# Local attention layers as a seven-stage pipeline on three rotating bank pairs, with the mask added by VectorE

## The reference, cut to what matters

```
x1 = global_attention(x) + x
y  = layernorm(x1)
for l in range(6):
    t = shift(y)                          # second 64 features come from the token before
    q, k, v = split(t @ Wqkv[l])          # 16 heads of 64
    q, k = l2norm(q)*qs, l2norm(k)*ks;  q, k = rotary(q), rotary(k)
    s = 8 * q_window @ k_window.T         # windows of 32 tokens see 32 before and themselves
    s = where(banned, -max, s);  a = softmax(s)
    y = y + (a @ v_window) @ Wo[l]
    n = layernorm(shift(y)) * g + b
    y = y + ((n @ W1a + b1a) * gelu(n @ W1g + b1g)) @ W2[l] + b2[l]
out = y + x1
```

## Time and profile before

| | |
|---|---|
| median of 3 runs | 3665.57 us (3654.13 to 3666.7) |
| profiled execution | 3663.69 us, its span 3661.9 us |
| TensorE | 3133.4 us busy, 86% of the span; mean granted clock 0.951 |
| VectorE | 2503.8 us, 68% |
| ScalarE | 2070.3 us, 57% |
| GpSimd | 2294.0 us, 63% |
| DMA | 71 GB/s mean; the main queue's packets take 32.4% of 16 engines |

### The profile page before, as it was taken

One profiled execution on the slowest core, in us unless ns is written; L12 is line 12 of the kernel. 1 busy time (PEld: TensorE's weight loads), 2 busy tenths in 40 slices (PEclk: granted clock), 3 DMA queues, 4 the chain that ended last, 5 costly groups with the idle time before them and its releaser, 6 DMA issues. The chain is left out here.

```text
span 3661.9 us, 121537 instructions
## 1 busy us (share of the span) xinstructions
PE 3133.4 (86%) x52983; PEld 2292.0 (63%) x52983; DVE 2503.8 (68%) x3404; ACT 2070.3 (57%) x2481; POOL 2294.0 (63%) x1606
## 2 busy tenths in 40 slices
PE   3499999999999999488888888888888888888885
PEld 2377777777777777256666666666666666666664
DVE  5777777777777774366676666766676667666673
ACT  2255555555555554256666666666666666666663
POOL 1545545454554540577777777777777777777772
PEclk7699999999999999699999999999999999999997
DMA  4645454544445450422223222322222232222221
GB/s 110 104 80 88 80 86 78 87 80 86 84 83 85 81 87 5 133 59 57 53 54 90 61 54 65 77 57 61 75 66 54 61 81 63 54 57 60 54 53 38
DMA packets 277481, 260.20 MB, mean 71 GB/s; under 512 B 106263, under 2 KB 220840, under 8 KB 276824
## 3 DMA queue, kind: packets, MB, share of 16 engines
q1 hardware_dynamic: 275272, 252.05, 32.4%
q10 hardware_dynamic: 1680, 0.40, 0.1%
HBM read 98.30 MB, written 40.37 MB: 38 GB/s over the span
## 5 line engine op out<-in xcount | busy, mean ns | idle before, releaser
L660 ACT ACTIVATE prob<-psS 128x1024 f32<-128x1024 f32 x512 | 524.2, 1024 | 603.0 <-PE psS L537 599.9
L824 DVE TENSOR_TENSOR colmax<-psS,colmax 128x1024 f32<-128x1024 f32 x480 | 587.2, 1223 | 315.3 <-PE psS L537 313.5
L537 PE MATMUL psS<-diag,pst 128*128 128x64 bf16 x16384 | 587.3, 195 | 13.9 <-issue 13.7
L537 PEld LDWEIGHTS psS<-diag,pst 128*128 128x128 f16 x16384 | 520.9, 99 | 74.1 <-issue 20.5
L1266 PE MATMUL R<-wqkv,xsT 128*128 128x512 f32 x1152 | 557.4, 607 | 1.5 <-ACT qT L1402 1.1
L529 PE MATMUL psS<-qst,kst 48*128 48x128 bf16 (+1 forms) x8192 | 382.8, 221 | 143.3 <-DMA pst<-p_parts 85.7
L758 POOL TENSOR_TENSOR rel<-rel,rec 128x1024 f32<-128x1024 f32 x64 | 151.8, 2372 | 510.5 <-DVE rec L837 510.5
L1530 POOL TENSOR_TENSOR pr<-pr,rnq 128x1024 f32<-128x1024 f32 x96 | 182.7, 1903 | 394.7 <-DVE pr L1611 394.7
L529 PEld LDWEIGHTS psS<-qst,kst 48*128 48x128 bf16 (+1 forms) x8192 | 235.6, 95 | 301.5 <-issue 156.6
L571 PE MATMUL psO<-prob,v 128*9 128x128 f32 x8192 | 326.3, 276 | 6.0 <-issue 5.4
L1266 PEld LDWEIGHTS R<-wqkv,xsT 128*128 128x128 f32 x1152 | 198.7, 192 | 164.1 <-issue 162.5
(11 more groups left out here) (190 smaller groups left out, 6341.9 us busy)
## 6 DMA issues: line engine op xcount, KB each, us to landing
v<-vs SPq DMA_DIRECT2D x576, 128.0 KB, 2.4
pst<-p_parts SPq DMA_DIRECT2D x512, 128.0 KB, 4.9
p_parts<-stage SPq DMA_DIRECT2D x64, 512.0 KB, 3.0
v<-vs SPq DMA_DIRECT2D x384, 64.0 KB, 2.0
wqkv<-in_L_ffn_Wqkv SPq DMA_DIRECT2D x18, 512.0 KB
q_stack<-qpart SPq DMA_DIRECT2D x6, 512.0 KB
qst<-q_stack SPq DMA_DIRECT2D x32, 96.0 KB, 5.2
wo<-in_L_ffn_Wo SPq DMA_DIRECT2D x6, 512.0 KB
```

The costliest lines, as they stand in the source:

```text
L537: last = pe.matmul(o, pst[:, par, g, P * jb:P * (jb + 1)], diag[:, par, g, h0:h0 + HH // 2, :], start=False, stop=(g == NG - 1), skip_grou ...
L660: act.activation(prob[:, st % 2, :], psS[:, slot_of("b", st)].rearrange("p a b -> p (a b)"), ACT.Exp)\
L824: dve.tensor_tensor(dst, src, dst, ALU.max).then_inc(a_read, 1)
```

## The change

- The local layers' program is written anew. Step s (from -1 to 101) works on seven units: projections, norms and rotation of s; key and query transposes of s-1; scores, softmax and weighted values of s-2; output transposes of s-3; output projection, residual and norm statistics of s-4; feed-forward 1 and gating of s-5; feed-forward 2 and residual of s-6. The transpose of the input of s+1 is in it as well.
- PSUM: three pairs of banks (`R[0]` to `R[2]`) are handed out in turn to ten uses a step (`RING`), in the order S, Q, kT, K, V, qT, pT, oT, h, O. Each use waits for the reader of the use three before it. The two remaining banks are `psA` (output projection, input transpose) and `psB` (normed input, feed-forward 2).
- The mask is added by VectorE, from PSUM into `pr` in SBUF. The maximum reads `pr` and the subtraction is done in place in `pr`. The two mask products go, and `pr` and q's rotated tile get two buffers.
- The input shift of a projection is done by ScalarE while it copies the transpose out (three copies, one of them a column carried to the next unit); its three DMAs go. The feed-forward shift stays three DMAs, into two buffers.
- Feed-forward 1 has the weights as the stationary side (six products of 128 columns). GELU takes its bias as a per-partition operand, and the bias and gating of the other half are one VectorE operation for each of three pieces. The three transposes, the bias add and the two copies behind them go. The bias comes as six column DMAs instead of one broadcast row.
- In the last layer x1's block is loaded, added by GpSimd and stored block by block. The final blocks go.
- Global attention: the `guard` event is at key block 11 instead of 12 (its DMAs behind block 12, not 13), `max1` is at 9 instead of 10, and VectorE takes events ahead of `a_max`.

```diff
-                ev[8], ev[10], ev[12] = "max0", "max1", "guard"
+                ev[8], ev[9], ev[11] = "max0", "max1", "guard"
...
+                    if jb > 0:
+                        take(unit_events(ul, first, last), jb - 1, it, ul, first, last)
                     if not (last and st + LEAD >= 4 * NB):
                         al, ja = divmod(st + LEAD, NB)
                         a_max(b + LEAD, st, al, ja)
-                    if jb > 0:
-                        take(unit_events(ul, first, last), jb - 1, it, ul, first, last)
...
+        RING = (("S", 2), ("Q", 0), ("kT", 1), ("K", 0), ("V", 0), ("qT", 1), ("pT", 2), ("oT", 3), ("h", 5), ("O", 2))
+        STEPS = range(-1, NT + 6)
+        turns = [(kind, s - lag) for s in STEPS for kind, lag in RING if 0 <= s - lag < NT]
+        slot = {t: i % 3 for i, t in enumerate(turns)}
+        earlier = {t: turns[i - 3] for i, t in enumerate(turns) if i >= 3}
+        read_by = {"S": "masked_done", "Q": "sqq_done", "kT": "kT_ready", "K": "sqk_done", "V": "v_ready", "qT": "qT_ready",
+                   "pT": "pT_ready", "oT": "oT_ready", "h": "g_done", "O": "o_ready"}
...
+    # TensorE, step s: S(s-2) Q(s) kT(s-1) K(s) wo(s-4) xnT(s-5) V(s) qT(s-1) xT(s+1) w2(s-6) pT(s-2) oT(s-3) h(s-5) O(s-2)
+                        pe.wait_ge(m["g_done"], n + 1)
+                        pe.wait_ge(m["xnT_ready"], min(n + 2, NT))
+                        for i, (lo, r) in enumerate(FC):
+                            last = pe.matmul(psB[:, 0:D], gT[0:r, i, :], w2[0:r, n // NB % 2, D * i:D * (i + 1)], ...)
...
+                        for a in range(2):
+                            for i, (lo, r) in enumerate(FC):
+                                last = pe.matmul(R[slot["h", n]][0:r, a, P * i:P * (i + 1)],
+                                                 w1[:, n // NB % 2, FF * a + lo:FF * a + lo + r], xnT[:], start=True, stop=True)
...
+    # ScalarE, step s: kT(s-1) square q(s) exp(s-2) square k(s) V(s) qT(s-1) pT(s-2) oT(s-3) gelu(s-5) xT(s+1)
+    # GpSimd, step s: scale k(s-1), root q(s-1), scale scores(s-2), add q(s), add k(s), xmb(s-6), table(s+1), root k(s), rstd(s-4)
...
+    # VectorE, step s
+                        dve.tensor_tensor(p, scores, allowed, ALU.add).then_inc(m["masked_done"], 1)      # s-2
+                        dve.tensor_reduce(mx[:], p, AX.X, ALU.max).then_inc(m["mx_done"], 1)
+                        dve.tensor_tensor(p, p, mx[:].unsqueeze(2).broadcast_to([P, LH, 2 * WIN]), ALU.subtract)
+                        rotate(n, 0, flat[slot["Q", n]], q1[:, n % 2, :], q2[:], "tq_done")               # s
+                        rotate(n, 1, flat[slot["K", n]], k1[:], k2[:], "tk_done")
+    # then: sum of q squares(s), residual(s-4), scale normed input(s-5), sum of exponentials(s-2), sum of k squares(s),
+    # reciprocal(s-2), residual(s-6), statistics(s-4), divide output(s-2), gate(s-5), normalize(s-4)
+                            last = dve.scalar_tensor_tensor(gT[0:r, i, :], R[slot["h", n]][0:r, 0, P * i:P * (i + 1)],
+                                                            b1_cols[0:r, n // NB % 2, i:i + 1], gl[0:r, i, :], ALU.add, ALU.mult)
+                        dve.tensor_scalar(xn[:], xs_f[:, n % 2, :], mv[:, 0:1], rstd[:, 0:1], ALU.subtract, ALU.mult)
```

More of the change, by code:

```diff
@@ L1257, in _, with free @@
             def _(pe):
-                def turn_x(n, par):
-                    wait(pe, xs_a_dma[par], (n // 2 + 1) * 48)
-                    pe.transpose(flat[1][:, 512:512 + P], xs_a[:, par, :], ident[:]).then_inc(m["xT_done"], 1)
-                def project(n, par, which, bank, done):
-                    w = at(wqkv, wp(n))
+                def free(kind, n):
+                    if (kind, n) in earlier:
+                        before, unit = earlier[kind, n]
+                        pe.wait_ge(m[read_by[before]], unit + 1)
@@ new lines, in turn @@
+                def turn(kind, n, src, done):
+                    o = flat[slot[kind, n]]
+                    for i in range(PAIRS):
+                        last = pe.transpose(o[:, P * i:P * (i + 1)], src[:, P * i:P * (i + 1)], ident[:])
+                    last.then_inc(m[done], 1)
+                for s in STEPS:
+                    n = s - 2
+                    if has(n):
+                        par = n % 2
+                        pe.wait_ge(m["qT_ready"], n + 1)
+                        pe.wait_ge(m["kT_ready"], n + 1)
+                        free("S", n)
+                        o = flat[slot["S", n]]
@@ new lines, in _ @@
+                        last.then_inc(m["s_done"], 1)
+                    n = s
+                    if has(n):
+                        pe.wait_ge(m["xT_ready"], n + 1)
+                        if n % NB == 0:
+                            pe.wait_ge(m["w_dma"], (n // NB + 1) * (16 * NWL))
+                        free("Q", n)
+                        project(n, 0, "Q", "q_done")
+                    n = s - 1
+                    if has(n):
+                        pe.wait_ge(m["kn_done"], n + 1)
+                        free("kT", n)
+                        turn("kT", n, kn, "kT_done")
@@ L1397, in _ @@
-                steps(pe, step)
+                                last = pe.matmul(o[WIN * w:WIN * (w + 1), P * i:P * (i + 1)], prT[:, i, WIN * w:WIN * (w + 1)],
+                                                 v2[:, par, w, :, i, :], start=True, stop=True, skip_group_check=True)
+                        last.then_inc(m["pv2_done"], 1)
             @block.scalar
@@ new lines, in _ @@
+                    n = s - 3
+                    if has(n):
+                        act.wait_ge(m["oT_done"], n + 1)
+                        if n > 0:
+                            act.wait_ge(m["wo_done"], n)
+                        copy(otT[:].rearrange("p a b -> p (a b)"), flat[slot["oT", n]], "oT_ready")
+                    n = s - 5
+                    if has(n):
+                        act.wait_ge(m["h_done"], n + 1)
+                        if n > 0:
+                            act.wait_ge(m["g_done"], n)
+                        for i, (lo, r) in enumerate(FC):
+                            last = act.activation(gl[0:r, i, :], R[slot["h", n]][0:r, 1, P * i:P * (i + 1)], ACT.Gelu,
+                                                  bias=b1_cols[0:r, n // NB % 2, 3 + i:4 + i])
+                        last.then_inc(m["gelu_done"], 1)
```

791 lines of the change are left out of this document (358 added, 433 removed).

## The result

| | median | ratio to before, 95% interval |
|---|---|---|
| before | 3659.85 us (3652.94 to 3666.7, 4 runs) | |
| after | 3406.81 us (3399.55 to 3418.45, 4 runs) | 0.9312 [0.9276, 0.9347] |

What follows compares the result with a forecast made beforehand. Interlocking engines bound the local step: chain and GpSimd loop 19.0 us, taken as 19.05, over TensorE's 17.2 floor. Periods -254, global attention -30, start -7, end -25, weight loads +4 sum to -312: 3352 us, range 3265 to 3490.

Steps and rivals of the forecast that it cites:

- the hold: Local step: GpSimd's power keeps VectorE's subtraction with two SBUF inputs waiting; with normalizing held up, 0.7 us a step.
- Bound and chain of the local step: Local step: TensorE floor 17.2 us; chain from scores through softmax, rotation and V to values 18.3 us without interference.
- rival 1: Local step: the power doesn't hold the port; 18.5 us a step, 3300 us in all; chance 20%.
- TensorE then has one gap: Local step: TensorE waits only once, before V's projection, for about 1 us.
- The part that the change adds unseen: Local softmax: the subtraction, now with two SBUF inputs, ends 1.08 us behind GpSimd's power, making the step 19.0 us.
- GpSimd closes the loop at the same length: Local step: the loop from q power through VectorE's work back to the next q power also takes 19.0 us.
- Global attention: -30: Global attention: earlier guard DMAs remove 29 us of waits, with a little clock: -30 us (0 to -45).
- Mask products gone: 0.52 of TensorE, in the floor: Local scores: dropping the two mask products saves TensorE 0.52 us a step, counted in its 17.2 us floor.
- Start, end, feed-forward shift, weight loads: Outside the local periods: start -7 us, end -25, weight loads +4; the feed-forward shift's 4.2 us of DMAs hidden.
- Rivals 2, 3 and 4: 2: bank waits and lower clock, 20 to 21.2 us a step, 25%; rival 3; 4: period stays 21 to 22, 3%.
- rival 3: Local step: TensorE falls to 1.2 GHz behind the gap before V; 27.8 us a step, about 4180 us; chance 4%.

Runs made afterwards that it cites:

- e6: e1 with GpSimd's q power ahead of the k scaling, so that the scaling runs beside the subtraction: 3426.19 us, one run.
- e5: e1 with the two mask products back on TensorE, maximum and subtraction reading PSUM: 3264.76 us, 0.8907 of before.
- e7: The kernel before with only the mask add moved to VectorE: 3867.25 us, 1.0543 of before.
- e1: The whole change with its global attention edits undone (old key blocks and event order): 3319.21 us, 0.9058 of before.

## Why the prediction was right and where it was wrong

The time was right by luck, since the terms missed by 101 and 57 us in opposite directions; the local step's chain was right but for the hold.

- **Bound and chain of the local step: right in the main.** V behind q's square and its order of events are in the trace as laid out (the subtraction starts 5.1 us behind the scores, laid out 5.0), and the clock is full. The chain came out at 18.5 by rival 1's sum and at 18.48 measured. "TensorE then has one gap" was wrong: the gate takes 0.85 us, not 0.6, and ends 2.2 us behind the scores' start, not 1.9, so that TensorE waits a second time, 0.46 us in 88 steps, for the bank that the gate reads.
- **"The part that the change adds unseen": failed.** The step said that the subtraction would be held by the power until 1.08 behind it. Its duration is 1.22 us in all 96 units, 94 of which start inside a power. Rival 1, given 20%, is what happened: 0.57 a step less than 19.05, 53 us over 94 periods, and the wait in front of V is 1.0 and not 1.5 to 1.7. The 1.08 is what e6 shows beside the scaling, but the proportion it is given with (0.55 to 0.75, of an operation of 1.22) makes 0.90, so that no row led to it. The Trainium skill (SBUF — State Buffer, "Who interferes with whom") has a GpSimd instruction that reads SBUF hold such a VectorE instruction for its whole length; the trace agrees for k scaling (1.95 us) and not for the power (1.22 us).
- **"GpSimd closes the loop at the same length": failed with it**, since that loop had the hold's rest in it.
- **"Global attention: -30": failed, and is the largest miss** (+71 in its place). The prediction priced what the earlier DMAs save (29 us, and that wait did go) and put the moved chain at nothing without a reason. What the runs showed in its place: L870 falls into L509 and takes 1.82 us for 0.17, and the column maximum behind it comes late. It had a row of this kind in hand, L829 held by GpSimd, and applied it to the local stage alone; that row has two SBUF inputs, though, and L870 has one, so it didn't show this case by itself. Of the 71, the column maximum's wait is +56 and the guard's -29. The other 44 weren't taken apart: waits that the profile puts down to "issue" grew from 24 to 40 us (L537, L529 and L571), and the granted clock from 300 to 1400 us is 0.97, where before had 0.99.
- **"Mask products gone: 0.52 of TensorE, in the floor": the size was right, the account was not.** It counted the saving on an engine that waits, and the 1.2 us of the add in the chain, but never set one against the other. Kept on TensorE, the mask saves 0.64 a step, 54 us (e5).
- **Start, end, feed-forward shift, weight loads: right** to 4 us each. VectorE does wait for the shift's DMAs (120.4 us in 89 times from 1600 to 3300 us), but it then waits for the values as well (157.6 us in 91 times), and TensorE never waits for them. No period is over 18.72 us, so the weight loads cost nothing that shows.
- **Rivals 2, 3 and 4** didn't occur. The lower clock that rival 3 feared came in the old pipeline, in e7, in nearly every step beside a new regular wait of TensorE (1.42 us). By 21.11 + 1.42 - 0.52 = 22.0 for a step at full clock, an estimate, it costs 1.9 of the 23.9 us, and not the 8.8 of the forecast.

## What to carry to other kernels

Before a short VectorE operation is moved, lay it beside GpSimd's timeline at its new place: a 0.17 us operation that fell into a 2.1 us one took up to 2.1, and all that was queued behind it waited. Price a move of work between engines by what the chain gains and loses, not by the engines' busy time: half a microsecond of TensorE was bought with 1.2 of the chain, for a loss of 0.64 a step. Then look which of TensorE's waits the longer chain makes, since such a wait can bring the lower clock as well (e7). A forecast that hits by offsetting errors is found out only by comparing the terms between fixed events.

## What the runs showed of the hardware that was not expected

- A GpSimd power over 128x16 (2.93 us) doesn't hold a VectorE operation with two SBUF inputs (1.22 us, in 94 of after's 96 units inside a power); a GpSimd multiplication over 128x1024 does (1.95 us, e6). In most units it starts some 2.1 us into the power; the one in e1 that starts 0.18 us into it (at 1555.44) takes 1.22 us too.
- VectorE operations over 8 elements per partition, a tensor_scalar (0.17 to 1.82 us), a cast (to 2.13) and a tensor_tensor (to 1.99), end 0.03 us behind the GpSimd operation that they fall into. A cast and a tensor_scalar have one SBUF tensor as input.
- A GpSimd memset, which only writes, holds the tensor_scalar as well (0.40 us).
- One more operation of 1.22 us on VectorE gave TensorE a new wait of 1.42 us a step and took the lower clock from 37 of 96 steps to 93 (0.97 to 0.93 in the local stage, e7). It cost 5.4% in place of the 3.2% of its own length over 96 units.
